# Layer 2 of a four-layer graph kernel: the halves of T made graph by graph and turned by one DMA, and a later place for the high half of x

## The reference

```python
Xw = X @ Wv + bv
sj = Xw @ aw[:d, 0]
si = Xw @ aw[d:, 0]
e = leaky_relu(sj[:, None, :] + si[:, :, None] + ab[0], negative_slope=0.2)
alpha_matrix = A * exp(e)
transition = alpha_matrix / (sum(alpha_matrix, axis=-1, keepdims=True) + 1e-12)
for k in range(3):
    H = H + Xk @ Wk[k] + bk[k]
    Xk = einsum('bij,bjd->bid', transition, Xk)
return relu(H)
```

## Time and profile before

| | us |
|---|---|
| median of 3 runs | 668.26 (666.8 to 669.39) |
| the profiled execution, its own time | 670.04 |
| its span in the trace | 668.2 |

### The profile page before, as it was taken

One profiled execution on the slowest core, in us unless ns is written; L12 is line 12 of the kernel. 1 busy time (PEld: TensorE's weight loads), 2 busy tenths in 40 slices (PEclk: granted clock), 3 DMA queues, 4 the chain that ended last, 5 costly groups with the idle time before them and its releaser, 6 DMA issues.

```text
span 668.2 us, 15857 instructions
## 1 busy us (share of the span) xinstructions
PE 623.1 (93%) x5014; PEld 452.0 (68%) x5014; DVE 560.8 (84%) x1712; ACT 526.6 (79%) x1191; POOL 376.5 (56%) x448
## 2 busy tenths in 40 slices
PE   5989999999999999898999979999999997999993
PEld 4667777777777776565666646666666664778882
DVE  3889998888888888778999888988988987688886
ACT  4667888877777777868999788787877785899995
POOL 1234556665555557756777435353535353899983
PEclk9999999999999999998999999999999998999998
DMA  9591338354646433344655334545453443487773
GB/s 271 182 233 48 80 65 221 79 145 82 149 87 150 86 65 63 63 81 89 103 110 98 63 75 85 111 81 109 83 110 83 103 87 64 81 188 188 180 188 127
DMA packets 174466, 76.14 MB, mean 114 GB/s; under 512 B 122160, under 2 KB 173872, under 8 KB 174384
## 3 DMA queue, kind: packets, MB, share of 16 engines
q1 hardware_dynamic: 164208, 66.34, 42.3%
q0 software_dynamic: 8448, 8.39, 8.5%
q10 hardware_dynamic: 1728, 0.40, 0.3%
HBM read 28.97 MB, written 8.39 MB: 56 GB/s over the span
## 4 chain that ended last, share of the span: by engine, by line
PE 30%; DVE 8%; POOL 6%; DMA 6%; ACT 3%; issue 2%; SPq 0%; ACTq 0%; POOLq 0%; DVEq 0%
PE banks L86 9%; PE banks L88 8%; PE banks L87 8%; DMA xT_lo<-x_halves 3%; DMA l_TT_lo<-l_T_lo 3%; DVE l_st L1057 2%; POOL x_halves L1143 2%; POOL l_rstd L1082 2%; PE banks L1237 2%; POOL l_U L2048 1%; PE banks L1605 1%; POOL l_T_lo L1845 1%; ACT l_t L1658 1%; DVE l_u L1762 1%; DVE l_rsum L1768 1%
## 5 line engine op out<-in xcount | busy, mean ns | idle before, releaser
L1091 ACT ACTIVATE x_resident<-l_pre,l_nmr,l_rstd 128x256 f32<-128x256 f32 x256 | 140.8, 605 | 7.7 <-POOL l_nmr L1085 7.7
L983 POOL TENSOR_TENSOR hq<-hq 128x512 f32<-128x512 f32 x48 | 71.7, 1493 | 90.9 <-ACT hq L690 88.6
L1143 POOL TENSOR_TENSOR x_halves<-x_resident,x_halves 128x1024 f16<-128x1024 f32 x46 | 98.1, 2133 | 16.5 <-DVE l_pre L1339 9.9
L1057 DVE BATCH_NORM_STATS2 l_st<-l_pre 128x6 f32<-128x256 f32 x256 | 93.3, 410 | 0.0
L86 PE MATMUL banks<-Wk_lo,xT_hi 128*128 128x512 f16 (+1 forms) x256 | 83.4, 326 | 3.3 <-DVE l_pre L1339 1.8
L87 PE MATMUL banks<-Wk_hi,xT_lo 128*128 128x512 f16 (+1 forms) x256 | 83.3, 325 | 0.0
L88 PE MATMUL banks<-Wk_hi,xT_hi 128*128 128x512 f16 (+1 forms) x256 | 83.2, 325 | 0.0
L1082 POOL TENSOR_TENSOR l_rstd<-l_veps,minus_half 128x4 f32<-128x4 f32 x64 | 71.7, 1121 | 15.1 <-DVE l_veps L1071 11.2
L86 PE MATMUL banks<-W2T_lo,h_hi 128*128 128x257 f16 x256 | 70.2, 274 | 3.5 <-DVE h_lo L849 1.3
L88 PE MATMUL banks<-W2T_hi,h_hi 128*128 128x257 f16 x256 | 70.1, 274 | 0.0
L87 PE MATMUL banks<-W2T_hi,h_lo 128*128 128x257 f16 x256 | 70.1, 274 | 0.0
(11 more groups left out here) (200 smaller groups left out, 1904.8 us busy)
## 6 DMA issues: line engine op xcount, KB each, us to landing
adj<-in_adj SPq DMA_DIRECT2D x32, 256.0 KB, 3.5
x_halves<-in_x SPq DMA_DIRECT2D x16, 512.0 KB, 4.3
x_resident<-b_half SPq DMA_DIRECT2D x8, 1024.0 KB, 7.9
x_resident<-in_x POOLq DMA_DIRECT2D x16, 512.0 KB, 5.9
out<-x_resident SPq DMA_DIRECT2D x15, 512.0 KB, 3.2
x_resident<-in_L_gnn_W SPq DMA_DIRECT2D x2, 512.0 KB, 5.5
x_resident<-in_L_gnn_Wk SPq DMA_DIRECT2D x1, 768.0 KB, 9.6
xT_hi<-x_halves SPq DMA_TRANSPOSE x48, 3.2
```

Of the source, the lines that this page charges most:

```text
L983: pool.tensor_tensor(hq[:, 0, :], hq[:, 0, :], hq[:, h, :], ALU.add).then_inc(hqs_ok, 1)
L1057: dve.bn_stats(L.st[p][:, j, :], L.pre[p][:, j, :]).then_inc(L.st_ok, 1)
L1091: act.activation(K.x[:, gcols(g, j)], L.pre[p][:, j, :], ACT.Identity, bias=L.nmr[p][:, j:j + 1], scale=L.rstd[p][:, j:j + 1]).then_inc(L. ...
L1143: pool.tensor_tensor(F.xs[p][1], x_group(K, g), F.xs[p][0], ALU.subtract).then_inc(F.x_lo, 1)
```

## The change

Five edits, all in layer 2, and no other layer is edited.

1. tf is gone. ACT's `T_high` makes the high half from u itself, one instruction for each graph (128 columns), with rinv as a per-partition scale.
2. `T_low` moves from POOL to DVE: four `scalar_tensor_tensor` instructions, u times rinv less the high half. They stand after the residuals of graphs 0 and 1.
3. The two halves of T lie side by side in one tile of 1024 columns, and SPq turns them by one DMA transpose in place of two.
4. In ACT's step `x_high` moves from between norm_apply 0 and 1 to right ahead of mid_high.
5. In DVE's step `norm_variance` moves from before far_low 2 and 3 (of the next group) to behind them.

```diff
-    tf = sb("tf", [128, C])
...
-    ts, tT = halves("T", [128, C]), [halves(f"TT{p}", [128, GP, N]) for p in range(2)]
+    both, turn = sb("T", [128, 2 * C], F16), [sb(f"TT{p}", [128, 2 * GP, N], F16) for p in range(2)]
+    ts, tT = [both[:, 0:C], both[:, C:2 * C]], [[t[:, 0:GP, :], t[:, GP:2 * GP, :]] for t in turn]
...
     def turned(eng, g, p):
 
-        eng.wait_ge(tT_in[p], 16 * (g - p) + 32)
+        eng.wait_ge(tT_in[p], 8 * (g - p) + 16)
...
         def transpose_T(g, p):
-            for s in range(2):
-                sp.wait_ge((t_hi, t_lo)[s], upto(g, 1, 1))
-                if s == 0 and reused(g):
-                    sp.wait_ge(out_ps, upto(g - 2, GP, GP))
-                sp.dma_start(tT[p][s][:], ts[s][:], transpose=True).then_inc(tT_in[p], 16)
+            sp.wait_ge(t_hi, upto(g, GP, GP))
+            sp.wait_ge(t_lo, upto(g, GP, GP))
+            if reused(g):
+                sp.wait_ge(out_ps, upto(g - 2, GP, GP))
+            sp.dma_start(turn[p][:], both[:], transpose=True).then_inc(tT_in[p], 16)
...
         def T_high(g, p):
-            act.wait_ge(tf_ok, upto(g, 1, 1))
+            act.wait_ge(rinv_ok, upto(g, 1, 1))
             if reused(g, 1):
                 turned(act, g - 1, 1 - p)
-            act.activation(ts[0][:], tf[:], ACT.Copy).then_inc(t_hi, 1)
+            for j in range(GP):
+                act.activation(ts[0][:, j * N:(j + 1) * N], S.u[:, j * N:(j + 1) * N], ACT.Copy,
+                               scale=rinv[:, j:j + 1]).then_inc(t_hi, 1)
...
@@ -1707,8 +1708,6 @@
                 T_high(0, 0)
             if has(-2):
                 norm_apply(K, L, act, g - 2, p, 0)
-            if halves_due(F, g + 2) and g >= 0:
-                x_high(K, F, L, act, g + 2, p)
             if has(-2):
                 norm_apply(K, L, act, g - 2, p, 1)
...
             if has(-2):
                 norm_apply(K, L, act, g - 2, p, 3)
+            if halves_due(F, g + 2) and g >= 0:
+                x_high(K, F, L, act, g + 2, p)
             if has(0):
                 mid_high(g, 0)
                 mid_high(g, 1)
...
             if reused(g, 1):
-                dve.wait_ge(tf_ok, upto(g - 1, 1, 1))
+                dve.wait_ge(t_hi, upto(g - 1, GP, GP))
+                dve.wait_ge(t_lo, upto(g - 1, GP, GP))
             dve.tensor_tensor(S.u[:], S.e[:], adjn[p][:].rearrange("p g n -> p (g n)"),
                               ALU.mult).then_inc(S.u_ok, 1)
...
-        def normalised(g):
-            u = S.u[:].rearrange("p (g n) -> p g n", g=GP)
-            dve.wait_ge(rinv_ok, upto(g, 1, 1))
-            if reused(g, 1):
-                dve.wait_ge(t_hi, upto(g - 1, 1, 1))
-                dve.wait_ge(t_lo, upto(g - 1, 1, 1))
-            dve.tensor_tensor(tf[:].rearrange("p (g n) -> p g n", g=GP), u,
-                              rinv[:, :, None].to_broadcast([128, GP, N]), ALU.mult).then_inc(tf_ok, 1)
+        def T_low(g, p):
+            if reused(g, 1):
+                turned(dve, g - 1, 1 - p)
+            for j in range(GP):
+                dve.wait_ge(t_hi, upto(g, GP, j + 1))
+                c = slice(j * N, (j + 1) * N)
+                dve.scalar_tensor_tensor(ts[1][:, c], S.u[:, c], rinv[:, j:j + 1], ts[0][:, c], ALU.mult,
+                                         ALU.subtract).then_inc(t_lo, 1)
...
         def step(g, p, has):
             q = 1 - p
-            if has(-1):
-                norm_variance(L, dve, g - 1, q, EPS)
             if g == -3:
                 far_low(0, 0, 0)
                 far_low(0, 0, 1)
@@ -1805,6 +1805,8 @@
             if has(1) and g >= 0:
                 far_low(g + 1, q, 2)
                 far_low(g + 1, q, 3)
+            if has(-1):
+                norm_variance(L, dve, g - 1, q, EPS)
             if has(0):
                 mid_low(g, 0)
                 mid_low(g, 1)
...
             if g == -2:
                 transition(0, 0)
                 row_sums(0)
-                normalised(0)
+            if g == -1:
+                T_low(0, 0)
             if has(1) and g >= 0:
                 transition(g + 1, q)
                 row_sums(g + 1)
-                normalised(g + 1)
             if has(0):
                 residual(g, p, 0)
                 residual(g, p, 1)
+            if has(1) and g >= 0:
+                T_low(g + 1, q)
+            if has(0):
                 norm_row(L, dve, g, p, 0)
...
     def gpsimd(pool):
-        def T_low(g, p):
-            pool.wait_ge(t_hi, upto(g, 1, 1))
-            if reused(g, 1):
-                turned(pool, g - 1, 1 - p)
-            pool.tensor_tensor(ts[1][:], tf[:], ts[0][:], ALU.subtract).then_inc(t_lo, 1)
-
         def step(g, p, has):
             q = 1 - p
             if halves_due(F, g + 2):
                 x_low(K, F, pool, g + 2, p)
-            if has(1):
-                T_low(g + 1, q)
             if has(0):
                 norm_scales(K, L, pool, g, p)
         return step, 2, 0
```

More of the change, by code:

```diff
@@ L1515, in layer2 @@
     hr = sb("hr", [128, GP, D])
-    rsum_ok, reps_ok, rinv_ok, tf_ok, t_hi, t_lo = map(
-        sem, ("rsum_ok", "reps_ok", "rinv_ok", "tf_ok", "t_hi", "t_lo"))
+    rsum_ok, reps_ok, rinv_ok, t_hi, t_lo = map(sem, ("rsum_ok", "reps_ok", "rinv_ok", "t_hi", "t_lo"))
     tT_in = [sem(f"tT_in{p}") for p in range(2)]
```

## The result

| | before | after |
|---|---|---|
| median of 7 runs each, us | 669.15 (666.8 to 669.75) | 675.65 (671.85 to 677.79) |
| ratio, 95% interval | | 1.0092 [1.0063, 1.0121] |
| profiled execution, own time / span, us | 670.04 / 668.2 | 673.24 / 671.3 |
| granted TensorE clock over the span | 0.989 | 0.989 |

The change costs 6.5 us by the medians, 6.2 by the ratio (4.2 to 8.1 by its interval); 5.0 were predicted.

What follows compares the result with a forecast made beforehand. TensorE was taken as the bound, with a floor of 10.89 us a step. The terms 3.8 + 0.25 + 0.9 - 0.2 + 0.3 gave +5.0 us, 673.3 us on the median; range 665.0 to 677.5 for 8 in 10.

Steps and rivals of the forecast that it cites:

- The x path is a loop without slack, and the variance goes on it whole: Layer 2, far projection through variance, x_low and xT_lo's DMA: a 10.89 us loop without slack; the later variance adds 0.57 us.
- 0.57 us a step: Layer 2's twelve steps from group 3 to 15: each grows from 10.89 to 11.46 us, +3.8 us in all.
- T's chain, r + 5.0, and its waits go: Layer 2: T lands 5.0 us after l_rinv's end (r), against 5.15 before; TensorE's waits for T vanish.
- the estimate by the Trainium skill: T's DMA: 256 KB lands at 2.6 us, 128 KB at 2.3; T's chain would gain 0.4 us.
- The seam, +0.9: Layer 1 to 2: group 0's T_low waits behind layer 1's last work; +0.9 us, bounds -0.5 and +1.5.
- the step from group 2 to 3: Layer 2, before the twelve steps: starts with some slack, so it pays only 0.25 us.
- x_high costs nothing: ScalarE, x_high ahead of mid_high: cost 0, covered by the 0.57 us stall; without cover up to 0.15 us a step.
- Disturbances +0.3: Layer 2: a loop without slack passes on each late DMA, some of which T hid before; +0.3 us.
- tail -0.2: Layer 2's last group: T lands 0.2 us earlier, so -0.2 us.
- Rival A: Layer 2: x path has slack, only waits for T count; -4.2 to -0.8 us, some 665.5 us; chance 0.25.
- Rival B: Layer 2: loop 0.3 us shorter than read, steps unchanged, seam +1 to +2; 670 us; chance 0.13, shared with another case.
- Rival C: Layer 2: VectorE becomes the bound, low halves 1.7 us, steps some 11.8 us; +9, 677 us; chance 0.07.

Runs made afterwards that it cites:

- Experiments 1 and 2: 1: after with the variance back ahead of far_low 2 and 3, 671.47 us; 2: before with only the variance moved behind them, 675.49 us.
- the third: After with x_high back between norm_apply 0 and 1; 677.33 us, ratio 1.0098.
- fourth: After with x_high back in its early place and GpSimd making x_low of the next group ahead of the norm scales; 699.04 us, ratio 1.0416.
- eighth: After with the variance back and GpSimd's x_low ahead of the norm scales, x_high left late; 672.82 us, ratio 1.0069.
- the sixth: After with VectorE's low halves of group 0's T moved ahead of layer 1's last four residuals; 674.39 us, ratio 1.0084.
- the fifth: After with the variance back and T's halves turned by two DMAs again; 671.91 us, ratio 1.0036.
- the ninth: After with the variance back, group 0's T made early and far_low 1 moved behind the variance; 669.96 us, ratio 1.0001.
- the eleventh: After with the variance back, group 0's T early, far_low 1 behind the variance and x_high back in its early place; 668.36 us, ratio 0.9979.

## Why the prediction was right, and where it was off

- *The x path is a loop without slack, and the variance goes on it whole:* right. Experiments 1 and 2 move it alone, one each way, and the steps go with it, 11.07 and 11.33.
- *0.57 us a step:* too much; the steps are 11.33 us, not 11.4 to 11.5, and TensorE idles 0.28 us for xT_lo, not 0.5. veps ends 1.12 us after the norm rows, as forecast 1.17, so 0.52 later. Of that 0.09 vanish at the other end: a product that TensorE is idle for starts 0.01 us after its weight load, where it stood 0.10 behind in the earlier trace rows. I had called that 0.10 part of the loop; it was slack. The mean growth over the floor is 0.47, and the twelve steps cost +2.6, not +3.8.
- *T's chain, r + 5.0, and its waits go:* the working holds. With r = 487.20 + 0.18, the low halves end at 487.96 + 1.13, r + 1.71 (r + 1.85 forecast), the DMA is issued at 489.16 and lands as a rule after 3.1 us, r + 4.9. Landings of up to 4.2 us leave 1.0 us of waits inside the layer. In the estimate by the Trainium skill (DMA: Bandwidth & Descriptors, "Anatomy of one DMA — SWDGE (gpsimd) path") 2.6 less 2.3 is 0.3, not 0.35, and the gain by it 0.5, not 0.4; the section is on DMAs that GpSimd issues, T's are SyncE's, and the rows have 3.1 and 2.5. The sum did not use it.
- *The seam, +0.9:* the term that was mis-sized most in the profiled execution. Up to group 3 it has +3.9, of which the step from group 2 to 3 is 0.24 (0.25 forecast) and the seam 3.7; the first experiment has +1.8 up to group 3. The mechanism was named, T_low behind layer 1's last group. T's DMA was even issued earlier than forecast (6.8 us behind the zero, not 7.9), since layer 1's four residuals take 1.68 us, not 2.66, with no T_low on GpSimd beside them; but it took 4.4 us to land, not 3.1 (3.0 in the first experiment, 3.2 in the third, whose VectorE has the order of after; why 4.4 is not shown). Above all I counted the delay of the walk alone (1.7 us, above my upper reading of 1.4) and not the clock behind it: 0.50 for over 6 us, a cost of 1.9. In the first, third, fourth and eighth kernels, with T late too, a window of 2 us at the same place shows 0.50 as well; in the sixth, with T early, none does. The wait for T alone does not decide it: TensorE idles 1.95 and then 1.29 us there in the fourth, 1.75 and then 1.25 in the fifth, and the fifth, whose T is late too, stays at 1.00.
- *x_high costs nothing:* right (experiment 3). Without the cover of the longer step up to 0.15 us a step were forecast; the ninth, with x_high late, has steps 0.05 us longer than the eleventh.
- *Disturbances +0.3, tail -0.2:* the twelve steps are 0.4 us over twelve of 11.33. The tail is not to be seen; the rest after group 15 is +0.1.
- The forecast had +3.8 and +0.3 for the twelve steps and +1.15 (0.25 and 0.9) up to group 3; the profiled execution has +2.6 and +3.9. There the total was near by luck, since two errors offset each other. That split is one execution's. By the ratios the variance costs 5.3 us (after less the first) and 4.9 (the second), where its terms were 3.8 and 0.25, and the late T 0.6 to 0.9, as forecast. Which of the two terms was too small in a typical execution stays open; the variance as the main cause does not depend on it. Rival A was wrong in its premise that the weight load's idle time is harmless. Rival B had the loop 0.3 us shorter than I read it; it was 0.09. Rival C did not come about, low halves at 1.13 us, though VectorE's u takes up to 1.14 us where it had 0.69, as x_low, 0.5 us late, runs into it (below).

## What to carry to other kernels

Before moving a small instruction, follow what waits for it until you come back to the same place in the next step: a loop as long as the bound engine's own work has next to no slack (here 0.09 us) though that engine's products show no wait. At a seam, give the late transfer its worst landing, and allow for a clock of 0.50 behind TensorE's idleness (here 1.7 to 1.9 us). Two engines that share SBUF ports are ordered against each other too, so place GpSimd's long reads beside VectorE's PSUM work.

## What the runs showed of the hardware that was not expected

An instruction of VectorE with two SBUF inputs stands still while GpSimd reads SBUF. Besides the fourth experiment's 2.48 us for 0.75, after itself shows it in two rows of its timeline: u, 0.69 us in every step of before, starts before x_low ends at 474.36 and ends 0.55 us behind it. In after and in the second, third and sixth kernels, all with V as in after, u takes 0.78 to 1.14 us in 9 to 13 of 14 steps; in all the others 0.69 or 0.68 throughout.

```profile
472.23 2.13 POOL L1143 TENSOR_TENSOR x_halves<-x_resident,x_halves 128x1024 f16<-128x1024 f32 x1
...
474.00 0.91 DVE L1764 TENSOR_TENSOR l_u<-l_e,adj 128x512 f32<-128x512 f32 x1 [0.26 <-ACT l_e L1703]
```
